# Cross-attention of a six-layer block on one core: keys dealt to the 32x32 squares by score chunk, a pair's transfers begun in two halves of eight, the last remainders shared by two engines

## The reference

```python
q = x1 @ Wq
k, v = jnp.split(x2 @ Wkv, 2, axis=-1)            # x2: ctx_1024, (2, 2048, 128)
q, k, v = map(_split_heads, (q, k, v))            # 16 heads of 64
attn = jnp.einsum('bhid,bhjd->bhij', q, k) * SCALE
attn = jax.nn.softmax(attn, axis=-1)
out = jnp.einsum('bhij,bhjd->bhid', attn, v)      # then Wo, bo
```

## Time and profile before

| | us |
|---|---|
| median of three runs | 459.5 |
| the profiled execution's own time | 458.62 |
| its span | 456.8 |
| TensorE busy in the span | 410.4 (90%) |
| VectorE | 336.6 (74%) |
| ScalarE | 271.2 (59%) |
| GpSimd | 232.9 (51%) |
| mean granted TensorE clock | 0.979 of full |

### The profile page before, as it was taken

How to read it: one execution, slowest core, us unless ns; L and a number is a source line. 1 busy time by engine, 2 the same in 40 slices (tenths; PEclk the granted TensorE clock), 3 DMA queues, 4 the chain that set the end, 5 groups by cost and what they waited for, 6 DMA issues and landing times.

```text
span 456.8 us, 8194 instructions
## 1 busy us (share of the span) xinstructions
PE 410.4 (90%) x3214; PEld 336.0 (74%) x3214; DVE 336.6 (74%) x498; ACT 271.2 (59%) x398; POOL 232.9 (51%) x138
## 2 busy tenths in 40 slices
PE   7996998999999999998898886999879999976896
PEld 6764787997978988887897453674657788854695
DVE  5798888897988899884224946804689999954664
ACT  4466758777677767667433363410169999962244
POOL 0022996987789978688730474100055664510024
PEclk9998899999999999999999997999999999998999
DMA  7728687768886776877971000699970000010000
GB/s 232 285 65 186 136 186 168 181 154 202 230 196 154 174 179 141 200 158 176 395 294 52 0 1 1 128 214 207 196 286 3 3 2 4 1 33 0 0 2 11
DMA packets 18645, 59.80 MB, mean 131 GB/s; under 512 B 5808, under 2 KB 7600, under 8 KB 16944
## 3 DMA queue, kind: packets, MB, share of 16 engines
q1 hardware_dynamic: 18608, 59.30, 50.9%
HBM read 19.30 MB, written 0.13 MB: 43 GB/s over the span
## 4 chain that ended last, share of the span: by engine, by line
PE 40%; DVE 16%; SPq 14%; issue 8%; POOL 7%; ACT 7%; DMA 7%; POOLq 0%; ACTq 0%; DVEq 0%
SPq L480 8%; POOL dT_lo L1268 6%; SPq L511 6%; PE ps L613 4%; DMA kstack<-k_lo 4%; PE ps L968 3%; PE ps L615 3%; PE ps L614 3%; PE ps L874 3%; PE ps L895 3%; DVE w_ring L1541 3%; PE ps L591 3%; PE ps L592 3%; PE ps L593 3%; DVE max L1393 3%
## 5 line engine op out<-in xcount | busy, mean ns | idle before, releaser
L1268 POOL TENSOR_TENSOR dT_lo<-z_sq,dT_hi 128x1024 fp32r<-128x1024 f32 x60 | 142.3, 2398 | 27.0 <-ACT dT_hi L997 26.9
L1063 ACT ACTIVATE y_sq<-ps,nmax 128x1024 f32<-128x1024 f32 x64 | 70.8, 1112 | 49.8 <-DMA z_sq<-y_sq 27.7
L1393 DVE TENSOR_REDUCE max<-ps 128x1 f32<-128x1024 f32 x64 | 77.7, 1214 | 18.5 <-PE ps L593 18.4
L613 PE MATMUL ps<-dT_hi,ctx_hi 128*128 128x256 f32 x256 | 74.9, 293 | 5.8 <-POOL dT_lo L1268 5.4
L1383 DVE STREAM_TRANSPOSE y_sq<-y_sq 128x1024 f32<-128x1024 f32 x60 | 74.1, 1234 | 2.3 <-ACT y_sq L1063 2.3
L615 PE MATMUL ps<-dT_hi,ctx_lo 128*128 128x256 f32 x256 | 72.3, 282 | 0.0
L614 PE MATMUL ps<-dT_lo,ctx_hi 128*128 128x256 f32 x256 | 72.3, 282 | 0.0
L1541 DVE SCALAR_TENSOR_TENSOR w_ring<-ps,neg_nbias,cap 128x1024 f32<-128x1024 f32 x56 | 67.6, 1276 | 3.6 <-PE ps L874 3.6
L1202 ACT ACTIVATE p_ring<-w_ring,nbias_sb 128x1024 f32<-128x1024 f32 x56 | 62.2, 1146 | 1.5 <-DVE w_ring L1541 0.8
L997 ACT ACTIVATE dT_hi<-z_sq 128x1024 fp32r<-128x1024 f32 x60 | 60.7, 1059 | 3.7 <-DMA z_sq<-y_sq 2.2
L591 PE MATMUL ps<-ctxT_hi,qk_hi 128*128 128x512 f32 x128 | 54.0, 422 | 7.7 <-ACT y_sq L1063 7.5
(11 more groups left out here) (209 smaller groups left out, 651.1 us busy)
## 6 DMA issues: line engine op xcount, KB each, us to landing
z_sq<-y_sq SPq DMA_DIRECT2D x240, 128.0 KB, 2.4
w_sb<-in_w SPq DMA_DIRECT2D x2, 2048.0 KB, 16.3
kstack<-k_hi SPq DMA_DIRECT2D x8, 512.0 KB, 11.1
kstack<-k_lo SPq DMA_DIRECT2D x8, 512.0 KB, 12.5
ctx_raw<-in_ctx_nat SPq DMA_DIRECT2D x2, 1024.0 KB, 8.4
ctxT_raw<-in_ctx_t SPq DMA_DIRECT2D x1, 2048.0 KB, 9.6
wg_sb<-in_wg SPq DMA_DIRECT2D x1, 1088.0 KB, 14.2
wu_sb<-in_wu SPq DMA_DIRECT2D x1, 1088.0 KB, 16.5
```

What stands on the lines that cost most here:

```text
L613: mm(acc, hi[:, k, :], dT_hi[m % 3][:, cols], start=(k == 0), stop=False)
L1063: nc.scalar.activation(out_t, keys, ACT.Exp, bias=nmax[:, hs % 2:hs % 2 + 1], scale=SCALE0, accum_out=rowsum[:, hs, p:p + 1]).then_inc(exp ...
L1268: nc.gpsimd.tensor_tensor(d_ring(dT_lo, m), z_chunk(m), d_ring(dT_hi, m), ALU.subtract).then_inc(d_lo, 1)
L1393: return v.tensor_reduce(max2[:, 2 * (hs % 2) + p:2 * (hs % 2) + p + 1], slot(2 * hs + p), AX.XY, ALU.max)
```

## The change

Four things are changed.

1. Quarter c of y_sq holds the keys of score chunk c (512 successive keys), so exp_half(hs, p) fills the two quarters 2p and 2p + 1 and no others, in their order. Within a quarter of z_sq the blocks are then taken as 4t + d instead of 4d + t, the context rows are loaded so that partition 32c + i holds keys 512c + 32k + i (`get_rows`: four DMAs with rows of 2 KB in the place of one with 8 KB), and the last pair's exponentials are written so that `turn` finds the same keys. `turn` waits for all four exponentials of the last pair.
2. The 16 transfers of a pair are issued as eight for quarters 0 and 1 behind the third transpose (`squared` at 4 pr + 3) and eight for quarters 2 and 3 behind the fourth, with a semaphore for each half. exp_half(hs, p) of an even head waits for half p only; d_round waits for both.
3. The remainders of chunks 53, 55, 57 and 59 are VectorE's (`ON_DVE`); the waits count accordingly (`rest_done`).
4. In copy_o the two halves' row sums are added by two tensor_scalar with a pointer in the place of one tensor_tensor.

```diff
+        def rest_done(m):
+            on_dve = sum(k <= m for k in ON_DVE)
+            return (d_lo_dve, on_dve) if m in ON_DVE else (d_lo, m + 1 - on_dve)
         def y_half(hs, p):
-            return y_sq[:, hs // 2 % 2, :, hs % 2, GRP // 2 * p:GRP // 2 * (p + 1)]
+            return y_sq[:, hs // 2 % 2, 2 * p:2 * p + 2, hs % 2, :]
         def z_chunk(m):
-            return z_sq[m // 4 % 3][:].rearrange("p a h (d t i) -> p d t (a h) i", d=4, t=4)[:, m % 4]
+            return z_sq[m // 4 % 3][:].rearrange("p a h (t d i) -> p d t (a h) i", d=4, t=4)[:, m % 4]
+        ON_DVE = (53, 55, 57, 59)
+            def get_rows(b, raw_t, s):
+                for c in range(4):
+                    rows = ins["ctx_nat"][:, b * NBLK + 4 * c:b * NBLK + 4 * c + 4, :]
+                    get(raw_t[32 * c:32 * c + 32, :].rearrange("i (k n) -> i k n", k=4), None, s,
+                        rows.rearrange("(k i) u d -> i k (u d)", k=4))
             for pr in range(NPR - 1):
-                sp.wait_ge(squared, 4 * pr + 4)
+                sp.wait_ge(squared, 4 * pr + 3)
...
                 for c in range(4):
+                    if c == 2:
+                        sp.wait_ge(squared, 4 * pr + 4)
                     for a in range(4):
                         sp.dma_start(z_sq[pr % 3][32 * c:32 * c + 32, a, :, :],
-                                     y_sq[32 * a:32 * a + 32, pr % 2, c, :, :]).then_inc(spread[pr % 2], 16)
+                                     y_sq[32 * a:32 * a + 32, pr % 2, c, :, :]).then_inc(spread[pr % 2][c // 2], 16)
...
             def turn(m):
-                pe.wait_ge(exped, 2 * NHS - 1 + d // 2)
+                pe.wait_ge(exped, 2 * NHS)
...
             def d_round(m):
-                act.wait_ge(spread[pr % 2], 256 * (pr // 2 + 1))
+                for p in range(2):
+                    act.wait_ge(spread[pr % 2][p], 128 * (pr // 2 + 1))
...
             def exp_half(hs, p):
-                if p == 0 and hs % 2 == 0 and pr >= 2:
-                    act.wait_ge(spread[pr % 2], 256 * (pr // 2))
-                if pr < NPR - 1:
-                    out_t = y_half(hs, p).rearrange("p c (k i) -> p k c i", k=HBLK)
-                    keys = slot(2 * hs + p).rearrange("p a (k c i) -> p (a k) c i", k=HBLK // 2, c=4)
+                if hs % 2 == 0 and pr >= 2:
+                    act.wait_ge(spread[pr % 2][p], 128 * (pr // 2))
+                out_t, keys = y_half(hs, p), slot(2 * hs + p)
+                if pr == NPR - 1:
...
             for m in range(ND):                    # gpsimd
+                if m in ON_DVE:
+                    continue
...
             def copy_o(pr):                        # vector
-                link(v.tensor_tensor(r, rowsum[:, 2 * pr:2 * pr + 2, 0], rowsum[:, 2 * pr:2 * pr + 2, 1], ALU.add))
+                for j in range(2):
+                    halves = rowsum[:, 2 * pr + j, :]
+                    s = v.tensor_scalar(r[:, j:j + 1], halves[:, 0:1], halves[:, 1:2], None, ALU.add)
+                link(s)
...
                 for m in (2 * (w + 1), 2 * (w + 1) + 1):
-                    if ND <= m < NCH:
+                    if m in ON_DVE:
+                        dve.wait_ge(d_hi, m + 1)
+                        rest(v, m).then_inc(d_lo_dve, 1)
+                    elif ND <= m < NCH:
                         e_rest(m)
```

More of the change, by code:

```diff
@@ L308, in build @@
         squared, d_hi, d_lo, pv_d = sem("squared"), sem("d_hi"), sem("d_lo"), sem("pv_d")
-        spread = (sem("spread0"), sem("spread1"))
+        d_lo_dve = sem("d_lo_dve")
+        spread = [[sem(f"spread{i}_{p}") for p in range(2)] for i in range(2)]
         u_copied, o_psum, o_copied = sem("u_copied"), sem("o_psum"), sem("o_copied")
@@ L459, in _ @@
             get(wk0_t[:, QUAD:, :], "wk0_t", "wqk1", ins["wk0_t"][:, QUAD:, :])
-            get(ctx_raw0[:], "ctx_nat", "ctx0", ins["ctx_nat"][:, 0:NBLK, :].rearrange("p k d -> p (k d)"))
+            get_rows(0, ctx_raw0, "ctx0")
             get(wv0[:], "wv0", "v0")
@@ L605, in weigh @@
                 if m < ND:
-                    pe.wait_ge(d_lo, m + 1)
+                    pe.wait_ge(*rest_done(m))
                 else:
@@ L626, in turn @@
                     for j in range(2):
-                        at = j * CTX + (4 * d + t) * P
+                        at = j * CTX + (4 * t + d) * P
                         last = nc.tensor.transpose(
@@ L1016, in split_n @@
                 hi_t, _, src = ctx_part(b, g)
-                act.wait_ge(load["ctx" + str(b)], 16)
+                act.wait_ge(load["ctx" + str(b)], 64)
                 copy(hi_t, src).then_inc(split_hi, 1)
@@ L1053, in exp_half @@
                 act.wait_ge(maxed, hs + 1)
-                if p == 0 and hs % 2 == 0 and pr >= 2:
-                    act.wait_ge(spread[pr % 2], 256 * (pr // 2))
-                if pr < NPR - 1:
-                    out_t = y_half(hs, p).rearrange("p c (k i) -> p k c i", k=HBLK)
-                    keys = slot(2 * hs + p).rearrange("p a (k c i) -> p (a k) c i", k=HBLK // 2, c=4)
[L1059 to L1062, removed]
+                if hs % 2 == 0 and pr >= 2:
+                    act.wait_ge(spread[pr % 2][p], 128 * (pr // 2))
+                out_t, keys = y_half(hs, p), slot(2 * hs + p)
+                if pr == NPR - 1:
+                    out_t = y_sq[:, pr % 2, :, :, :].rearrange("p c h n -> p (c h n)")
+                    out_t = out_t[:, hs % 2 * CTX:(hs % 2 + 1) * CTX].rearrange("p (k c i) -> p c k i", k=NBLK, c=4)
+                    out_t, keys = out_t[:, 2 * p:2 * p + 2], keys.rearrange("p c (k i) -> p c k i", k=NBLK)
                 nc.scalar.activation(out_t, keys, ACT.Exp, bias=nmax[:, hs % 2:hs % 2 + 1], scale=SCALE0,
@@ L1266, in _ @@
             for m in range(ND):
+                if m in ON_DVE:
+                    continue
                 pool.wait_ge(d_hi, m + 1)
-                nc.gpsimd.tensor_tensor(d_ring(dT_lo, m), z_chunk(m), d_ring(dT_hi, m), ALU.subtract).then_inc(d_lo, 1)
+                rest(nc.gpsimd, m).then_inc(d_lo, 1)
                 step = m // 2 + LAG - 1
@@ L1278, in _ @@
             pool.wait_ge(turned, 4)
-            pool.wait_ge(d_lo, ND)
+            pool.wait_ge(*rest_done(ND - 2))
             nc.gpsimd.memset(vx[:, :, :, DC:DC + 1], 1.0)
```

9 lines of the change are left out of this document (6 added, 3 removed).

## The result

The changed kernel takes 449.6 us (median of 4 runs, 449.4 to 450.5), against 459.6 us for the kernel before beside it: ratio 0.976, 95% interval 0.973 to 0.979. The forecast was 450.5. The medians of the first comparison differ by 10.0 us, those of the second by 8.1, and the two profiled spans by 8.0 (456.8 and 448.8), so some 8 to 9 us are the change and the rest is scatter. Medians and ratios in this document leave out two executions that lay far above the others of their kernels, one of 460.4 us (row sums by one tensor_tensor) and one of 2236 us (the last kernel).

A forecast was written before the change was run, and what follows sets the result against it. TensorE was taken as the bound, its standstills as the gain: -5.0 - 1.8 - 2.1 = -8.9 us from 458.62 gives 449.7, with 0.9 for the runs' median 450.5 us; range 447.0 to 455.5.

The forecast's parts named there:

- The steady part, -5.0: Layer 0 cross-attention: transfers begun eight and eight remove TensorE's stops for exponentials and remainders; -5.0 us, between -2 and -6.3.
- What I left over: Steady part of layer 0 attention: 1.3 us allowed for waits that stay, from a slow landing or GpSimd's context splits.
- The rival of GpSimd or late second halves holding as before: Steady part: GpSimd or the second eight transfers hold ScalarE, only 1.5 of 5.0 us come back; 454.0 us, chance 0.15.
- The context rows, 0 (0 to +2): Context loads at start and pair 6: three more 0.6 us issues each, shifting pair 7's first transfers up to 1.8 us; 0.
- The start, -1.8: Start of layer 0 attention: head 4's exponential, GpSimd's first remainder and the first weighing come earlier; -1.8 us.
- The first rival: Gaps before the first weighing: TensorE's clock falls to half for 7 us, costing 3.5 us; 454.0 us, chance 0.20.
- The gap of 1.5 us alone: Before scores(5,1): TensorE's new gap; a present gap of 1.49 us before 209.45 was cited as not followed by half clock.
- The row sums, 0 (0 to -2): copy_o on VectorE: two tensor_scalar cost about 0.3 us, pair load falls from 11.5 to about 11.0; no gain alone.
- The tail, -2.1: Last eight remainders of layer 0 attention, shared by VectorE and GpSimd: about half of 4.1 us returns; between +1 and -4.1.
- The waits that I said would stay: Tail: last pair's first transpose waiting for four exponentials, about 0.9 us; weighing of chunk 54 held by ScalarE, about 1.1.
- Strides, 0: Exponentials and transposes in the new key order: no cost; transposes bounded at -0.1 to +0.5 us each.
- The slower rival: VectorE's 60 transposes take longer in the new stride: 468 us at 0.6 us more each, chance 0.05.

The follow-up runs named there:

- the second: The changed kernel timed again beside the kernel before, six runs, in the follow-up study: 451.2 against 459.3 us, ratio 0.981.
- the last kernel: Changed kernel with second context's rows loaded in halves, 5 calls of zero matmuls before the first weighing, GpSimd's two small instructions moved behind chunk 41: 446.2 us, ratio 0.971.
- the two kernels without the stop: Changed kernel with second context's rows in two halves (449.8 us), or with each context in one transfer, wrong key order (449.6 us).
- the second profile: Another profiled execution of the unaltered changed kernel, with a 6.8 us half-clock spell; that kernel timed again took 451.2 us, ratio 0.981.
- the kernel with 7 calls of zeros: Changed kernel with 7 calls of zero matmuls on a free bank in TensorE's gap before the first weighing: 449.5 us, ratio 0.978.
- 22 calls of zeros: Changed kernel with 22 calls of zero matmuls before the first weighing, which filled 9.3 us: 455.8 us, ratio 0.990.
- The kernel with all transfers late: Changed kernel with all 16 transfers of a pair begun behind its fourth transpose again: 457.4 us, ratio 0.995.

## Why the prediction was right

**The steady part, -5.0.** Right. Nine of ten stops went, 6.3 us of stops before and 1.48 after, so 4.9 us. What I left over was 1.3 us, and 1.48 stayed, in one place. A pair takes (196.01 - 40.35)/13 = 11.97 us from pair 2's first exponential to pair 15's, where I had said 12.0; undisturbed ones take 11.73. The rival of GpSimd or late second halves holding as before is refuted: the second eight land in time everywhere but once.

**The context rows, 0 (0 to +2).** The term that was mis-sized. I counted the issues, 0.6 us each, and looked for who stands behind them. They moved pair 7's first transfers by 0.5 us. What cost was time in the DMA engines, of which the load in four transfers takes more, so that transfers behind it landed after up to 7.1 us. From the first weighing to the stage end the first profile of the changed kernel takes 1.7 and 1.9 us more than the two kernels without the stop, all three with a spell of 3.4 us at half clock, and 1.48 of it is the stop itself (1.09 in the second profile). It hid in the 1.3 that I left over for a slow landing. The bound of +2 was about right.

**The start, -1.8.** The first weighing came at 47.87 (47.44 the second time), forecast 47.4, so 1.35 and 1.8 us earlier than before; the stop in front of it is 3.37 us, as said.

**The clock.** The first rival came true in its mechanism and not in its price: of nine profiles of the changed kernel and its variants with the gap of 3.4 us at the start, the clock fell near it in eight, and stayed at 1.00 in the one with all remainders on GpSimd, where nothing at that place differs. In six of the eight the spell lasts 3.4 us and costs 1.6, not 3.5: I took over the 7 us of the earlier trace rows. In the other two it lasts 6.8 us, as in the kernel before, and there it costs 2.4 (second profile), in which its first 0.7 us fall into the gap itself and the stop behind the context load is 0.3 us shorter than in the kernel with 7 calls of zeros. The gap of 1.5 us alone does nothing, also as said: it is there with 7 and with 22 calls of zeros as well, and the clock stays at 1.00.

**The row sums, 0 (0 to -2).** Right for the sum by itself (1.001 alone), and low in company: 1.6 us where the transfers no longer set the pace, within the bound of -2. The reading of its cause, VectorE held until GpSimd's running instruction is over, held in every row looked at.

**The tail, -2.1.** Measured 2.3. The waits that I said would stay are 0.91 + 0.71 us against 0.9 + 1.1.

**Strides, 0.** Transposes 1225 to 1239 ns, exponentials 1098 to 1122. The slower rival never reached its condition.

The sum, -8.9, met -8.3 at the stage end and -8.0 in the spans. That it fits so closely is luck. From the measured parts it reads -4.9 for the stops, -1.35 for the start, -2.3 for the tail, +1.6 for the clock and -1.6 for the row sums, -8.5 in all: the clock, which I had as a rival, and the row sums, which I had at 0, cancel.

## What to carry to other kernels

When a transfer between two buffers of the same engine chain sets the pace, start the part of it whose inputs are ready, and give each part its own semaphore: the order of the data in the buffer decides whether that can be done. A load that is cut into pieces for this has to be judged by what the DMA engines move of it in a microsecond and by how busy they are already, not only by its number of issues. Line up single profiles at an event that both share before comparing where they end.

## What was not expected of the hardware

- The hold between VectorE and GpSimd works both ways. The Trainium skill ("GPSIMD Engine Reference", Specifications) names contention with VectorE's instructions that have two SBUF inputs; the rows here agree and show its size. VectorE's remainder took 1.21 us when free and up to 3.12 when held, ending 1.08 us after GpSimd's; GpSimd's took 3.06 and 2.72 us instead of 2.37 to 2.40 when VectorE's had begun first.
- Around the context loads the kernels with four transfers of 32 partitions in runs of 2 KB moved 214 GB/s at 108 to 114 us and 219 and 234 in the first 18 us, where the one with a transfer of 128 partitions in runs of 8 KB moved 267 and 281, at similar DMA shares.
- A spell at 1.2 GHz isn't of one length. Around gaps of 3.4 to 3.6 us it lasted 3.4 us in six profiles of nine of the changed kernel and its variants, 6.8 us in two, and there was none in one; the kernel before has 6.8 us. The kernel with all transfers late has a second spell between its two long stops, 6.8 us again.
- One execution of five of the last kernel took 2236 us with TensorE busy 99% of it at a recorded clock of 1.00. I have no cause for it; none of the others did this.
